# Layer 0 of a graph network: the sparse block moves to directly behind the aggregation on TensorE, the next one-hots to ahead of the residuals on VectorE

## What is computed

```
h = x @ W                                  # 3125 x 256
deg = segment_sum(ones, col);  dinv = where(deg > 0, rsqrt(deg), 0)
norm = dinv[row] * dinv[col]               # an added self loop per node
out = segment_sum(h[row] * norm, col) + b
x = layernorm(x + relu(out))
# layer 1 begins with products of the new x:
x = layernorm(x + (segment_sum(x[src] * w, dst) @ W_rel.T + b_rel + x @ W_root.T))
```

## Time and profile before

| what | us |
|---|---|
| median of 3 runs (1624.96 to 1625.32) | 1625.16 |
| the profiled execution, its own time | 1622.16 |
| its span, first to last instruction | 1620.3 |
| PE busy in the span | 1441.5 (89%) |
| DVE busy in the span | 1178.8 (73%) |
| POOL busy in the span | 915.3 (56%) |

### The profile page before, as it was taken

One profiled execution on the slowest core, in us unless ns is written; L12 is line 12 of the kernel. 1 busy time (PEld: TensorE's weight loads), 2 busy tenths in 40 slices (PEclk: granted clock), 3 DMA queues, 4 the chain that ended last, 5 costly groups with the idle time before them and its releaser, 6 DMA issues.

```text
span 1620.3 us, 36657 instructions
## 1 busy us (share of the span) xinstructions
PE 1441.5 (89%) x12043; PEld 1162.7 (72%) x12043; DVE 1178.8 (73%) x3034; ACT 489.3 (30%) x909; POOL 915.3 (56%) x913
## 2 busy tenths in 40 slices
PE   4869999999997999999588888888888879999998
PEld 4648778777775888887366566666666657888887
DVE  9788898888863344445599999999999979443443
ACT  0342222222210101003355555555554546100000
POOL 0148455554454556563577777777777710456774
PEclk9989999999999999999599999999999979999999
DMA  9985455445566565541344444444444441766652
GB/s 206 107 154 175 163 167 178 139 167 166 182 230 212 173 209 189 172 142 51 88 114 111 113 111 113 112 114 112 112 114 112 112 141 68 262 210 227 198 155 80
DMA packets 132297, 241.49 MB, mean 149 GB/s; under 512 B 70300, under 2 KB 94976, under 8 KB 125968
## 3 DMA queue, kind: packets, MB, share of 16 engines
q0 software_dynamic: 45024, 128.68, 28.6%
q1 hardware_dynamic: 87087, 110.47, 22.8%
HBM read 193.42 MB, written 50.96 MB: 151 GB/s over the span
## 4 chain that ended last, share of the span: by engine, by line
PE 49%; POOL 17%; issue 12%; DVE 9%; DMA 8%; SPq 2%; ACT 1%; DVEq 1%; POOLq 0%
PE bank L1736 16%; POOL ring L706 16%; PE bank L1684 7%; PE bank L1618 7%; PE bank L1610 3%; PE bank L1663 3%; PE bank L1868 3%; DMA edge_rows<-edge_list 3%; PE bank L1636 2%; DMA ring<-attention_rows,work 2%; PE bank L1745 2%; PE bank L1603 1%; DVE work L1122 1%; DMA big<-rows_layer,big 1%; POOL big L661 1%
## 5 line engine op out<-in xcount | busy, mean ns | idle before, releaser
L706 POOL DMA_INDIRECT ring<-attention_rows,work x420 | 398.3, 948 | 150.1 <-issue 145.5
L661 POOL DMA_INDIRECT big<-rows_layer,big x304 | 289.2, 951 | 265.0 <-issue 238.5
L657 POOL DMA_INDIRECT ring<-rows_layer,ring x152 | 156.8, 1032 | 162.7 <-PE bank L1663 123.4
L1868 PE MATMUL bank<-work,ring 128*65 128x48 f32 x3360 | 240.4, 233 | 8.2 <-ACT work L871 7.3
L1868 PEld LDWEIGHTS bank<-work,ring 128*65 128x65 f32 x3360 | 229.6, 148 | 16.7 <-ACT work L871 14.2
L871 ACT ACTIVATE work<-work 128x960 f32<-128x960 f32 x84 | 161.6, 1924 | 84.3 <-DVE work L1415 83.3
L1736 PE MATMUL bank<-big,ring 128*128 128x256 f32 x750 | 164.2, 379 | 0.0
L1736 PEld LDWEIGHTS bank<-big,ring 128*128 128x128 f32 x750 | 142.5, 190 | 19.5
L1736 PE MATMUL bank<-big 128*128 128x256 f32 x664 | 145.9, 379 | 0.0
L1684 PE MATMUL bank<-big 128*128 128x256 f32 x608 | 139.3, 384 | 7.3 <-DMA big<-rows_layer,big 7.2
L1736 PEld LDWEIGHTS bank<-big 128*128 128x128 f32 x664 | 126.1, 190 | 17.7 <-ACT big L895 0.4
(11 more groups left out here) (254 smaller groups left out, 2312.0 us busy)
## 6 DMA issues: line engine op xcount, KB each, us to landing
adjacency<-big SPq DMA_DIRECT2D x16, 1600.0 KB, 6.5
big<-adjacency SPq DMA_DIRECT2D x16, 1600.0 KB, 8.5
ring<-adjacency SPq DMA_DIRECT2D x16, 1600.0 KB, 7.1
ring<-attention_rows,work POOLq DMA_INDIRECT x420
rows_layer<-big SPq DMA_DIRECT2D x50, 128.0 KB, 2.8
edge_rows<-edge_list SPq DMA_DIRECT2D x1, 4983.0 KB
big<-rows_layer,big POOLq DMA_INDIRECT x304, 3.3
rows_layer<-big SPq DMA_DIRECT2D x5, 960.0 KB, 10.5
```

What stands on the lines that cost most here:

```text
L657: G.indirect_dma_start(out=rows0[:, s, :], out_offset=None, in_=y0tab[:, :], in_offset=bass.IndirectOffsetOnAxis(ap=src_l0[j][:, c:c + 1], ...
L661: G.indirect_dma_start(out=rows1[:, s, :], out_offset=None, in_=(y1tab if q < 2 * LAYER else y3tab)[:, :], in_offset=bass.IndirectOffsetOn ...
L706: G.indirect_dma_start(out=rows[0:EP, s, c, 0:ZG], out_offset=None, in_=ztab[:, :], in_offset=bass.IndirectOffsetOnAxis(ap=idx[:, g, c:c + ...
L1868: ins = mm(sum_banks[k % 3][0:FH, h * WIN:(h + 1) * WIN], rows[0:EP, s, c, h * FH:(h + 1) * FH], prob[:, k % 2, c, h * WIN:(h + 1) * WIN], ...
```

## The change

On PE `scatter0` of the step moves from behind the first `turn_x_next` to directly behind `aggregate`, ahead of the first `relate` and of the wait for `c_dig`. On DVE `next_hots0` moves to ahead of the first `residual`, so that all residuals follow it. In step 15, where there are two blocks, the second call of `next_hots0` and of `scatter0` stay behind. Nothing is added or removed.

```diff
@@ VectorE, end of a step
                 for m in summed0(k):
                     sums0(m, k)
-                for m in summed0(k - 2)[:1]:
+                for q in after0.get(k, [])[:1]:
+                    next_hots0(q)
+                for m in summed0(k - 2):
                     residual(m)
-                for q in after0.get(k, []):
+                for q in after0.get(k, [])[1:]:
                     next_hots0(q)
-                for m in summed0(k - 2)[1:]:
-                    residual(m)
@@ TensorE, end of a step
                         aggregate(i)
                 relating, turning = summed0(k - 2), summed0(k - 1)
+                if k < ND:
+                    scatter0(after0[k][0])
                 for m in relating[:1]:
                     relate(m)
...
                 for m in turning[:1]:
                     turn_x_next(e0, m, order0[m])
-                if k < ND:
-                    scatter0(after0[k][0])
                 for m in relating[1:]:
                     relate(m)
```

## The result

The changed kernel takes 1650.88 us (median of 4 runs, 1649.79 to 1651.58) where the kernel before, beside it, takes 1625.06 us (4 runs, 1624.46 to 1625.32). The ratio is 1.0163 with a 95% interval of 1.0143 to 1.0182: 25.8 us slower. The profiled execution of the changed kernel took 1649.79 us with a span of 1648.0.

The account below looks back on a forecast made before the run. The prediction took PE, busy 263.19 of 272.05 us in layer 0's loop, as the bound. Tails and steps (17.3 + 1.2 + 0.3 + 3.0 = 21.8 us) plus 6.7 for the clock gave 1653.7 us, range 1644.0 to 1660.5.

Parts of the forecast that it names:

- The odd tail: Layer 0, steps 3 to 13: `init0` waits for DVE's line 1157, one more `relate` follows; 2.89 us each, 17.3 us.
- Step 15 and step 1: Last step: 1.2 us after block 16's wait for rows; first odd step: one later turn, 0.3 us.
- The even tail: Layer 0, seven even steps: scatter starts at once, two adjacent turns wait for ACT's copy; +0.43 us each, 3.0 us.
- DVE's edit: One-hots ahead of residuals on DVE: worth nothing found; the gap ahead of line 1192 is no wait for the scatter.
- rival 3: Gap ahead of line 1192 truly waits for the scatter and DVE sets the pace: faster, 1616.1 us; chance 0.03.
- The clock: PE's clock falls to 0.50 behind some odd-step stalls, 1.67 us each; four of seven taken, 6.7 us.
- rival 2: PE's clock falls behind all seven odd-step stalls: 21.8 + 11.7, 1658.7 us; chance 0.08.
- Rival 1: PE's clock holds in all stalls, only the fixed part of 21.8 us: 1647.0 us; chance 0.13.
- The sum: Whole kernel: fixed part 21.8 plus clock 6.7, 28.5 us slower, 1653.7 us.
- rival 4: DVE reads the sparse bank 2.9 us earlier, PE's move costs nothing: about 1625 us; chance 0.04 including anything missed around zero.

Follow-up runs that it names:

- early read: DVE's line 1157 moved to the end of the preceding even step's tail, against the changed kernel: 1637.23 us, ratio 1.0057; with TensorE's half alone: 1637.11 us, 1.0062.
- relate-first kernel: Kernel before with the scatter moved ahead of the `c_dig` wait and first turn but behind the first `relate`, DVE unchanged: 1630.92 us, ratio 1.0021.
- TensorE's half: Kernel before with only PE's scatter moved directly behind the aggregation, DVE's order unchanged: 1656.63 us, ratio 1.0192.
- second execution: The changed kernel run once more, same program, against the kernel before: 1655.15 us, ratio 1.0162.
- odd-only kernel: Kernel before with PE's scatter moved directly behind the aggregation in odd steps alone, DVE unchanged: 1650.40 us, ratio 1.0157.
- VectorE's half: Kernel before with only DVE's next one-hots moved ahead of all residuals, PE unchanged: 1637.84 us, ratio 1.0073.
- even-only kernel: Kernel before with PE's scatter moved directly behind the aggregation in even steps alone, DVE unchanged: 1634.25 us, ratio 1.0055.
- early read in the kernel before: Kernel before with only DVE's line 1157 moved to the end of the preceding even step's tail: 1627.45 us, ratio 0.9996.

## Why the prediction was right, and where it was off

**The odd tail.** Right in mechanism and size: `init0` waits for line 1157 (2.17 us measured, "some 2.2" expected), the two `relate` are 2.90 us apart (2.89), the tail is 11.05 us ("about 11.0"). Over six steps without the two falls it is 21.1 - 3.3 = 17.8 us, 2.97 each, where the prediction had 17.3. The early read shows that the stall is what it was said to be, and the relate-first kernel shows which piece of work covered it.

**Step 15 and step 1.** +1.5 us against 1.2, and, with the fall of the kernel before taken out, 6.55 - (7.99 - 1.67) = +0.23 us against 0.3.

**The even tail.** +0.36 us each in place of +0.43: 2.5 us in seven steps, not 3.0. The new wait for ACT's copy is there, 0.61 us where the pair at the end of layer 0 had 0.55. DVE was not late in step 6 of the changed kernel, and behind all even tails only 0.1 us a step is lost. In TensorE's half alone it was late, and 0.4 us a step is lost there.

**DVE's edit "is worth nothing that I can find".** Right about the gap: it stayed, so rival 3 (faster) is out. Wrong as a sentence on the edit by itself. Alone it costs 10.9 us in the loop, which the prediction did not see because it asked what the one-hots gain, and not, for odd steps, who waits for a residual behind them. Together with TensorE's half it saves about 1.8 us in the loop, which the prediction had at nothing. In the changed kernel's odd tails its price is hidden: the stall delays PE until the one-hots are over, and it came out when the early read took the stall away.

**The clock** is the term that was mis-sized. The prediction took four falls, 6.7 us. The price of one is right: 12.72 - 11.05 = 1.67 us. But two came, and the one of step 1 that the kernel before paid was missing, which the prediction did not count as a possible gain. Net it is one fall, 1.7 us. In the second execution it is three, less one. Falls followed 2 of the 8 stalls of 2.2 us (steps 1, 3, ..., 15) in one execution and 3 of 8 in the other. The rule that the prediction took from the Trainium skill ("TensorE: Matmul & The Clock Gate", section "HAM oscillation — how this bites in real kernels") would have no fall behind gaps of this length. This case's traces differ, and the measurement decides. Nor did it fall in all, so rival 2 is out. Rival 1, with 21.8 us, was nearer to the 23.9 us of the trace than the point with 28.5.

**The sum.** Without falls: 17.8 + 2.5 + 0.2 + 1.5 + 0.2 = 22.2 us, predicted 21.8. With the net fall 23.9, predicted 28.5. So the trace has the clock term 5.0 us too high and the rest 0.4 us too low, 4.6 us together. The medians differ by 25.8, 1.9 us more than the traces show for the change; where these lie is not shown. They are why the point is only 2.8 us too high: that part is luck.

**No difference** (rival 4) needed DVE's read 2.9 us earlier. With it moved into the step before, the loop was still 9.8 to 11.2 us longer than that of the kernel before: the even steps' cost remains, and in odd ones the two `relate` stand together.

No version beats the kernel before: the best order of the scatter tried here is the old one, and the early read is worth nothing measurable there (0.9982 to 1.0010).

## What to carry to other kernels

Before moving a block of work to the front of an in-order engine, ask what its first instruction waits for and which work covers that wait now; here one product of 1.9 us covered most of it. Ask too what stood apart because of the block: two products that share a bank, or two turns, cost their full chain through the other engines once nothing lies between them. And an edit on the engine that is not the pace can save 1.8 us beside one order of the other engine and cost 0.7% beside another, so its price is to be asked again for each order of its partner.

## What the runs showed of the hardware

Stalls that are the same to 0.01 us are followed by a granted clock of 0.50 for 3.4 us or by none, and the same program differs between executions: falls at steps 5 and 9, then at 1, 7 and 13; in TensorE's half at 1, 5, 9 and 13; in the odd-only kernel at none, with the same stalls. The gap of 1.86 to 1.88 us in step 1 was followed by a fall in the kernel before and in VectorE's half, and by none in the even-only kernel and with the early read in the kernel before. Each fall that hit a scatter cost 1.67 us. What decides stays open.

A gap stands ahead of line 1192 in every order tried, with changing names for the releaser (the scatter, or "issue"). In steps 2 to 15 it is 0.68 to 0.85 us where a `residual` stands directly ahead of it (1.11 to 1.18 in step 6), and 0.98 to 1.09 us where none does (1.42 in step 6). That it belongs to the start of that loop on DVE, and runs in part behind the `residual`, is argued from this; which of its instructions takes the time, and why step 6 has more, no run here shows.

The stretch ahead of the loop varies as well: the first aggregation began at 119.65 us in the kernel before and between 120.97 and 126.27 us in the others. From 80 us to there the mean granted clock was 0.83 in the kernel before, 0.75 in the changed one and 0.74 in the even-only and odd-only ones. For a change inside one loop, the loop's own length in the trace was the sharper measure.
